# A decoder's retention stage on one Trainium2 core: its opening reordered on GpSimd and VectorE, and its weights loaded in two parts

## What is computed

```python
def _forward(x, q_w, q_b, k_w, k_b, v_w, v_b, g_w, g_b, o_w, o_b):   # x: layer-normalised
    q = x @ q_w + q_b
    k = (x @ k_w + k_b) * SCALING
    v = x @ v_w + v_b
    g = x @ g_w + g_b
    ...                                   # 16 heads
    qr = _theta_shift(q, sin, cos)        # q * cos + rotate_every_two(q) * sin
    kr = _theta_shift(k, sin, cos)
    qk = jnp.einsum('bhmd,bhnd->bhmn', qr, kr) * mask
    qk = qk / denom
    out = jnp.einsum('bhmn,bhnd->bhmd', qk, vr).transpose(0, 2, 1, 3)
    out = (out - mu) / jnp.sqrt(var + 1e-05)
    out = jax.nn.silu(g) * out
    return out @ o_w + o_b
```

## Time and profile before

| | |
|---|---|
| median of 3 runs | 972.23 us (970.29, 972.23, 976.11) |
| the profiled execution | 973.3 us, of which the profile's span is 971.3 us |
| instructions | 22991 |
| TensorE busy | 823.8 us (85% of the span) |
| VectorE busy | 771.3 us (79%) |
| ScalarE busy | 650.1 us (67%) |
| GpSimd busy | 380.5 us (39%) |

### The profile page before, as it was taken

The page is one execution under the profiler, slowest core; times in us unless marked ns, Lnnn a source line. Parts: engine busy times, 40 slices in busy tenths (PEclk is TensorE's granted clock), DMA queues, the critical chain, the costliest instruction groups (busy, mean ns, idle before and its releaser), DMA issues. The chain is left out here.

```text
span 971.3 us, 22991 instructions
## 1 busy us (share of the span) xinstructions
PE 823.8 (85%) x9198; PEld 535.7 (55%) x9198; DVE 771.3 (79%) x1404; ACT 650.1 (67%) x1155; POOL 380.5 (39%) x384
## 2 busy tenths in 40 slices
PE   1287779798768879999978999998889978999998
PEld 0123223233235746556544676766778865788787
DVE  7999989934678998888776999998799986667443
ACT  4579698987658555545227888887789866656431
POOL 1043435241227504000015878878375622324220
PEclk9998889988859999999999999999999999999999
DMA  5401506060051003000013000000255650000000
GB/s 156 87 2 20 68 7 83 1 88 1 1 174 45 2 27 138 1 1 2 1 30 149 2 3 3 3 2 3 77 88 104 110 83 1 1 12 12 12 23 33
DMA packets 58505, 40.22 MB, mean 41 GB/s; under 512 B 42320, under 2 KB 54814, under 8 KB 57248
## 3 DMA queue, kind: packets, MB, share of 16 engines
q1 hardware_dynamic: 55648, 36.14, 17.2%
q10 hardware_dynamic: 2752, 2.62, 0.9%
HBM read 19.09 MB, written 2.10 MB: 22 GB/s over the span
## 5 line engine op out<-in xcount | busy, mean ns | idle before, releaser
L598 ACT ACTIVATE t_pT<-t_sc 128x1536 f32<-128x1536 f32 x96 | 136.8, 1454 | 29.0 <-PE t_sc L705 28.7
L278 POOL TENSOR_SCALAR_AFFINE_SELECT t_pT<-t_pT 128x512 f32<-128x512 f32 x64 | 75.6, 1202 | 167.9 <-ACT t_pT L598 167.9
L705 PE MATMUL t_sc<-t_qk 32*128 32x512 f16 (+3 forms) x1152 | 89.4, 366 | 46.8 <-DMA t_qk<-t_sin_parts 26.6
L705 PEld LDWEIGHTS t_sc<-t_qk 32*128 32x128 f16 x1152 | 37.1, 99 | 106.8 <-issue 51.2
L726 PE MATMUL t_ot<-t_pT,t_v 128*17 128x512 f32 (+3 forms) x768 | 81.6, 537 | 11.1 <-DVE t_ou L442 5.0
L2855 POOL TENSOR_SCALAR_AFFINE_SELECT r_att<-r_att 128x1024 f16<-128x1024 f16 x64 | 68.7, 1099 | 26.9 <-DVE r_att L2904 26.9
L2064 PE MATMUL c_pso<-ck_VO,c_pT 128*128 128x256 f16 x480 | 55.1, 273 | 5.2 <-DMA c_pT<-c_ph 4.4
L2354 ACT ACTIVATE m_sg<-m_psg 128x512 f32<-128x512 f32 x32 | 19.1, 596 | 55.5 <-PE m_psg L2397 55.5
L2064 PEld LDWEIGHTS c_pso<-ck_VO,c_pT 128*128 128x128 f16 x480 | 46.5, 98 | 11.4 <-DMA c_pT<-c_ph 5.4
L1968 ACT ACTIVATE c_pt<-c_pss,c_mx 128x154 f32<-128x154 f32 x128 | 48.6, 406 | 2.8 <-DVE c_mx L1859 2.8
L2418 PE MATMUL m_acc<-gw_down,m_hp 128*128 128x256 f16 x384 | 47.2, 273 | 2.5 <-DVE m_hp L2310 2.0
(11 more groups left out here) (631 smaller groups left out, 2408.0 us busy)
## 6 DMA issues: line engine op xcount, KB each, us to landing
t_qk<-t_cos_parts SPq DMA_DIRECT2D x24, 128.0 KB, 5.1
t_qk<-t_sin_parts SPq DMA_DIRECT2D x24, 128.0 KB, 6.6
x<-in_x ACTq DMA_DIRECT2D x4, 512.0 KB, 7.1
out_x<-x SPq DMA_DIRECT2D x8, 256.0 KB, 2.1
r_rcos<-in_ret_cos SPq DMA_DIRECT2D x1, 1280.0 KB, 8.4
r_rsin<-in_ret_sin SPq DMA_DIRECT2D x1, 1280.0 KB, 10.0
t_qk<-t_cos_parts SPq DMA_DIRECT2D x16, 64.0 KB, 2.7
gw_raw<-in_gateT SPq DMA_DIRECT2D x1, 1024.0 KB, 8.3
```

The costliest lines, as they stand in the source:

```text
L278: last = g.affine_select(out=blk, in_=blk, compare_op=ALU.is_ge, fill=0.0, base=0, pattern=[[0, 4], [1, P]], channel_multiplier=-1)
L598: a.activation(pT[:, at:at + 3, :].rearrange("p a s -> p (a s)"), sc[s % 2][:], ACT.Exp, scale=CURVE * CURVE / math.sqrt(2 * DH)).then_inc ...
L705: last = t.matmul(sc[s % 2][:, 512 * k + at:512 * k + at + w], qk[r, g % 3, 1, of_k, P * i:P * i + P], qk[r, g % 3, 0, of_q, q0:q0 + w], s ...
```

## The change

It does five things. GpSimd's list in the retention starts with `id16` and goes straight on to tile 0's `swap`; `v16` and `rowtile` are filled behind that swap in step -2, the power of tiles 12 to 15 is taken in step 0, and the next stage's constants are made in step 1. TensorE's first transposes wait for `id16` alone; the wait for `v16` stands before `delta`, that for `rowtile` before ScalarE's `expand`. VectorE's list starts with step -2; the statistics of tiles 12 and 13 come behind `rotate(1)`, those of 14 and 15 behind `rotated_low(1)`, and `spread` behind `values_low(0)`, all in step -1. The shift of tiles 12 to 15 is made in step 2 instead of 1. In the experts' stage `load` is cut in two: the five weights are issued when four of the six halves are split, the rest after all six, as before. The number of arithmetic instructions and of DMAs is the same.

```diff
         @block.sync
         def _(sp):
+            sp.wait_ge(lent.low_done, 4)
+            ahead.load_weights(sp, ins)
             sp.wait_ge(lent.low_done, 6)
-            ahead.load(sp, ins)
+            ahead.load_rest(sp, ins)
...
-    def load(self, sp, ins):
+    def load_weights(self, sp, ins):
         sp.dma_start(self.rawo, ins["L1_attn_o_w"].rearrange("(c p) n -> p c n", p=P)).then_inc(self.s_o, 16)
         n = 0
         for nm, w in (("q", 256), ("k", 256), ("v", 512), ("g", 512)):
             sp.dma_start(self.raw[:, :, n:n + w], ins[f"L1_attn_{nm}_w"].rearrange("(c p) n -> p c n", p=P)).then_inc(self.s_w, 16)
+            n += w
+
+    def load_rest(self, sp, ins):
+        n = 0
+        for nm, w in (("q", 256), ("k", 256), ("v", 512), ("g", 512)):
             sp.dma_start(self.last[:, n:n + w], ins[f"L1_attn_{nm}_w"][D - 1:D].broadcast_to((P, w))).then_inc(self.s_last, 16)
             n += w
...
         @block.gpsimd
         def _(g):
             own = Tally(g, s_g)
-            own.link(g.memset(rowtile[:], 0.0))
-            for h in range(4):
-                own.link(g.memset(rowtile[32 * h:32 * h + 32, h:h + 1], 1.0))
             own.link(g.memset(id16[:], 0.0))
             g.affine_select(out=id16[:], in_=id16[:], compare_op=ALU.not_equal, fill=1.0, base=0,
                             pattern=[[-1, P]], channel_multiplier=1).then_inc(s_c, 1)
-            g.memset(v16[:, :, 0, :, VD:VC], 1.0).then_inc(s_c, 1)
-            g.memset(v16[:, :, 1, :, VD:VC], 0.0).then_inc(s_c, 1)
-            ahead.power(g, 2)
-            opening.constants(g, own)
...
                 swap(s + 2)
+                if s == STEPS[0]:
+                    g.memset(v16[:, :, 0, :, VD:VC], 1.0).then_inc(s_c, 1)
+                    g.memset(v16[:, :, 1, :, VD:VC], 0.0).then_inc(s_c, 1)
+                    own.link(g.memset(rowtile[:], 0.0))
+                    for h in range(3):
+                        own.link(g.memset(rowtile[32 * h:32 * h + 32, h:h + 1], 1.0))
+                    g.memset(rowtile[96:128, 3:4], 1.0).then_inc(s_c, 1)
+                    g.wait_ge(s_c, 4)
+                if s == 0:
+                    ahead.power(g, 2)
+                if s == 1:
+                    opening.constants(g, own)
                 power(s - 1)
                 split_state(s)
...
         @block.vector
-            ahead.statistics(v, own, 12, NT)
-            ahead.spread(v, own, 2)
...
-                if s == STEPS[0] + 3:
+                if s == 2:
                     ahead.offsets(v, 2)
                 gate(s - 2)
                 rotate(s + 2)
+                if s == -1:
+                    ahead.statistics(v, own, 12, 14)
                 low(s, 1)
                 rotated_low(s + 2)
+                if s == -1:
+                    ahead.statistics(v, own, 14, NT)
                 values_low(s + 1)
+                if s == -1:
+                    ahead.spread(v, own, 2)
...
                     if t == 0:
-                        a.wait_ge(s_c, 3)
+                        a.wait_ge(s_c, 4)
...
                     if n == 0:
-                        t_.wait_ge(s_c, 3)
+                        t_.wait_ge(s_c, 1)
...
                     t_.wait_ge(swapped, t + 1)
+                    if t == 0:
+                        t_.wait_ge(s_c, 3)
                     wait(t_, kept_state, t)
```

## The result

| | before | changed |
|---|---|---|
| median, 18 runs each, same chip | 971.18 us (969.38 to 976.11) | 974.64 us (972.00 to 977.15) |
| the profiled execution | 973.3 us, span 971.3 | 976.8 us, span 975.1 |
| TensorE, VectorE, ScalarE, GpSimd busy | 823.8, 771.3, 650.1, 380.5 us | 824.6, 775.6, 650.7, 375.6 us |

The ratio is 1.0027, with a 95% interval of 1.0016 to 1.0039: the changed kernel is 2.6 us slower (1.6 to 3.8; the two medians lie 3.5 apart). That is under the 0.5% that the forecast named as the least one measurement can tell, but it goes the other way than the forecast, which had the kernel 1.4 us faster, at 970.8, and 974.64 is 0.6 us above the range's end of 974.0.

What follows compares the result with a forecast made beforehand. It took the retention's opening, a chain of waits starting at GpSimd's late swap, as the pipeline's clock. Terms: 2.0 - 0.35 - 0.3 = 1.35 us sooner; on the median, 972.23 - 1.4 = 970.8 us, range 967.5 to 974.0.

Steps and rivals of the forecast that it cites:

- the last term of the change's sum: Experts' stage: earlier folds on GpSimd land beside VectorE's work, cost 0.3 us, a third of one 0.98 us collision.
- the forecast's own signs of being wrong: Among them: a `low` or turn in the experts' block 0 waiting over 1 us, or `low(0, 0)` still waiting for ScalarE.
- VectorE then waited 1.25 us for TensorE anyway: Experts' stage: why the one `m_hp` held 0.98 us beside a fold had cost nothing in the kernel before.
- the folds hit the tile chain: Rival, experts' block 0: folds hold four `L866` and TensorE waits, 3.9 us paid instead of 0.3, 974.5 us; chance 0.10.
- its point of decision, 1.65 us: Fold rival, experts' block 0: it decides from a cost of 1.65 us, two hits, on.
- The opening: Retention's start: GpSimd's earlier swap and VectorE's new order let `low(0, 0)` start 2.0 us sooner, 1.7 at half clock.
- as chosen: Retention's opening: TensorE's values taken at full clock, 1.46 us, rather than half clock, 2.77 us.
- Step 2: Retention: the later constants and shift delay the product that waits for `power(0)`, cost 0.35 us, bounds 0.2 and 1.0.
- more than forecast: Rival: constants fit a wait, folds cost nothing, ScalarE's earlier casts help step 0; gain 3.0 us, 969.2 us; chance 0.16.

Runs made afterwards that it cites:

- weights_only: The kernel before with only the change's split load, the five weights issued sooner; 975.84 us, ratio 1.0038 to the kernel before.
- the two junk kernels: `folds_held` plus unused GpSimd work where the early folds lay: twelve fills (971.17 us, ratio 0.9978) or six subtractions (976.15 us, ratio 1.0028).
- folds_held: The changed kernel, early loads kept, but GpSimd's folds wait for the second expert's down projection in block 0; 972.67 us, ratio 0.9997.
- filling: Kernel before with GpSimd's new order, plus useless matmuls in TensorE's waits: experts and retention 971.00 us, ratio 0.9982; experts only 971.97 us, ratio 0.9985.

## Why the prediction was wrong

**The step that failed** is the last term of the change's sum: "I take 0.3 (a third of one collision; bounds 0 and four collisions, 3.9)". Measured alone, in `weights_only`, it is 3.7 us (2.0 to 5.3). The mechanism was named and its unit was right: one fold beside one `m_hp` or L866 costs 0.98, and the two L866 of the changed kernel lost 1.97 together. TensorE, which waits for them, stood still 3.68 us there; a wait of over 1 us at such a turn was among the forecast's own signs of being wrong. The count was wrong, for a reason that stood in the forecast's own numbers. It had the folds start "some 3 to 6 us sooner" (they did, 6.1), and then priced them as if they had moved by about one microsecond, against the one row at 371.94. Six microseconds before 373.12 is 367.0, and VectorE's timeline of the kernel before has there:

```profile
366.93 0.73 DVE L861 TENSOR_SCALAR ce_room<-x,mr_sm 128x256 f32<-128x256 f32 x2
367.73 0.92 DVE L866 TENSOR_TENSOR ce_room<-ce_room 128x256 f16<-128x256 f32 x2
...
370.66 0.73 DVE L861 TENSOR_SCALAR ce_room<-x,mr_sm 128x256 f32<-128x256 f32 x2
```

With the last L866 at 371.94 these are both pairs of tiles. The folds take 8 us (364.60 to 372.72), so they could not miss the first pair. The second pair, with the L866 at 371.94 that the forecast named, got away in the changed kernel: the delay had moved it behind the folds, to 374.83, and its rows have their old lengths (0.73 and 0.92). What the forecast left out is that not only L866 is exposed: L861, the tiny L847 and the `m_hp` ahead of them lost as much for each instruction, and in the changed kernel's profile six instructions are hit. The upper bound of 3.9 was near the value to take, and as a bound it was too low for that one execution (4.8 of waiting).

The other half of that step also failed: "VectorE then waited 1.25 us for TensorE anyway" was true of one `m_hp` behind the last tile, and I let it stand for the block. The rows of the tiles have TensorE waiting behind them, so nothing there absorbed the delay; and an `m_hp` at an earlier place made TensorE wait 0.89 us in `weights_only`.

**The rival** "the folds hit the tile chain" was the one that came. It gave 974.5, 2.3 us above the kernel before, and 974.64 was measured, 2.6 above; its point of decision, 1.65 us, was passed by far. That the time fits so well is partly luck: it priced four L866, and what was hit were two L866, two L861, L847 and an `m_hp`, with two falls of the clock in that profile. The argument against it, that two of the four L866 may escape, came true, by the second pair; but a count of L866 alone was the wrong count, and the chance of 0.10 was too low. The Trainium skill's rule ("SBUF — State Buffer", "Who interferes with whom"), under which every such overlap blocks, is borne out by the two junk kernels: 0.15 (L847) and 0.74 us (the two L866) beside fills, 1.22 and 1.82 beside reads.

**The opening** was right in its chain and a little small in size: forecast 2.0 sooner at the first score part, measured 2.4. `spread` took 1.40 (517.25 to 518.65), as forecast, and the values were at full clock, as chosen. The 0.4 more came in two pieces, each against the block's start: the rotation's low part 0.2 sooner than forecast (5.00 against 5.20), the statistics and `values_low` 0.24 closer behind it, since an instruction here starts up to a tenth before the one ahead of it ends (515.40 to 517.25 is 1.85, where I put three times 0.70). What the forecast had not counted is that the fall of the clock would come later and not go: 0.9 us was lost between the third and the fourth score part and 0.4 at the fifth. In the sum the retention gained 1.1 us, the forecast said 2.0 - 0.35.

**Step 2** was put at 0.35 and cost nothing that a row shows.

**The range** ended at 974.0. It "holds most of the fold case" only if that case is taken below its own price; with the rival at its own 974.5 the end had to lie above 975. The runs before also reached 3.9 us above their median, and only 1.8 was allowed. In the case "more than forecast" the 0.35 is added to a 2.0 that never had it taken off; its 3.0 and 969.2 come out from the sum of 1.35 plus 0.35, 0.3 and 1.0.

## What to carry to other kernels

A transfer that lands sooner moves the work that waits for it, and that work lands beside something: lay its whole length, not its first instruction, over the trace of before, shifted by the full gain, and count every VectorE instruction in it that the two can hold up and that TensorE waits for, at the place to which the delay itself moves it. Nobody waited for these folds, so the earlier start had nothing to win. In a chain of waits put first what the chain needs: moving one instruction pair past ten small entries gave all of the 2.4 us at the first score part, and the second engine's reordering nothing on top.

## What the runs showed of the hardware

- A VectorE instruction that is held up by a GpSimd subtraction pays for up to the remainder of that instruction, whatever its own size: 128 x 4 numbers went from 0.15 to 1.22 us (366.34 to 367.56, beside a fold that ends at 367.54), 128 x 256 rose by 0.98 each, 128 x 512 by 1.10, beside folds of 1.28 us. GpSimd is held up in turn: in `folds_held` a fold took 2.26 us (from 374.49) beside a two-input VectorE instruction of 128 x 1024 that had started at 373.32, against 1.27 for the fold with nothing of the kind beside it.
- L861, which has one tensor operand, is held up by GpSimd's subtractions (1.67 to 2.70 us for two, against 0.73) and slightly by fills (1.01 and 1.13). The Trainium skill ("SBUF — State Buffer", "Who interferes with whom") counts this kind among those that can take both ports, and the fills agree with it; L847 and L866 show nothing beside fills.
- The granted clock fell to 0.50 for some 3.4 us at a time, and once, in the changed kernel's profile, for 6.8. The falls came behind stretches in which TensorE had waited much, but not behind each: the wait of 3.08 us at the experts' start was followed by a fall in ten of the eleven profiles without filling there, and by none in `weights_only`. With GpSimd's new order and no filling in the retention the fall lay some 15 us into the block in seven profiles and at 7.5 in two, and in none was it gone; with filling it was gone, in one profile. What a fall costs depends on what lies under it: 1.3 us on a projection that VectorE waits for (2.72 us in place of 1.46), nothing that could be seen when it lay some 8 us into the experts, 0.7 when it lasted twice as long there. How much of the change's loss in block 0 is wait and how much is clock varies between executions: 3.3 us of wait alone in `weights_only`; 4.8 of wait and 2.4 beside two falls in the changed kernel's profile.
- Not tried: folds at a place where VectorE has no two-input work for TensorE, which could make the early loads harmless, though no row shows anything that they would win.
